# Row transposes that wait for each bank of the values by itself, and a value addition ahead of its slot's maxima

## The chip, the core and the metric

The kernel runs on one core of a Trainium2 chip, in one launch. The core's engines work side by side and each takes its own instructions in order: TensorE (PE, matrix products and transposes; its weight loads are shown apart as PEld), VectorE (DVE), ScalarE (ACT), GpSimd (POOL), and SyncE (SP), which issues DMAs. They wait for each other by semaphores. The metric is the device time of a launch in microseconds. A run is compared by its time, and the profiled execution is a run of its own.

## The reference: what is computed

16 images of 256 x 256 give 256 rows each (an edge filter of 2 x 2, clipped), and 77 text tokens are looked up as further rows, so that a batch element has 333 rows of 256. Then comes a layernorm, windowed attention with 16 heads of 16, a residual, a second layernorm and a mixture of eight experts, of which each row takes two.

```python
h = concatenate([tok(x), table[x_txt]], axis=1)
y = layernorm(h)
q, k, v = split_heads(y @ Wq + bq), split_heads(y @ Wk + bk), split_heads(y @ Wv + bv)
# windows of 128 rows at 0, 64, 128, 192, and a last one that ends at the last row
scores = q_win @ k_win.T * scale + pos_bias
merged = (sum over the windows of softmax(scores) @ v_win) / (windows that hold the row)
h = h + merged @ Wo + bo
x2 = layernorm(h)
top_scores, sel = top_k(softmax(x2 @ gate_w.T), 2)
h = h + scatter_add(top_scores * expert(sel)(x2))     # expert: (silu(x2 @ w1) * (x2 @ w3)) @ w2
```

## The kernel before, in words

There are two stages. The first goes over the 16 batch elements and does attention, the router, and the scattering of rows to the experts' slots in DRAM. The second (after about 740 us) works through the experts' tiles.

The first stage is a software pipeline in steps b = -3 to 17. In one step b the engines attend to batch element b, finish the element before it (b - 1: output projection, residual, second layernorm, router) and prepare the next ones (b + 1: q, k and v; b + 2: first layernorm; b + 3: image filter). Each step has 20 slots k, one for each group of four heads in each of five windows. The slot is the unit in which every engine's code is written: each engine has a loop over k, with the attention work of the slot and, hung on certain k, a piece of the other work. The order within each engine is therefore as it is written; no scheduler moves anything.

A group's attention work passes through the engines one or more slots apart: PE makes the scores of slot k (line 1105) into one of two banks of `s_bank`; DVE adds the bias and takes the negated maxima (line 818, four times, one per head, each with a short read of the accumulator; it signals `max_ready` after the fourth); ACT takes the exponentials of slot k - 1 (line 703, four times); PE transposes the probabilities of slot k - 3 (line 1116) into `t_bank`; ACT (line 696), for every fourth group DVE (line 827), copies them to `probsT`; PE multiplies those of slot k - 4 by the values (line 1132). PE's scores of slot k wait for the maxima of slot k - 2.

The work around the change happens in slots 12 to 18 and shares `m_bank`, two PSUM banks:

- PE makes the values of element b + 1 in three products (`v_proj`, line 1083): windows 0 and 2 into the two halves of bank 0 of `m_bank` (slots 12, 13), window 4 into bank 1 (slots 14, 15).
- DVE adds the bias `bv` to each and writes it to the values' tile (`add_v`, line 806, on the tile `v_all`). Each addition increments `v_ready`: the first two stand in slot 14 of DVE's code, the third in slot 16.
- In slot 15 DVE normalises the rows of element b - 1 (line 773, three instructions that write `rows`), once POOL has its inverse roots; in slot 16 those of element b + 2 (line 773, `xn`).
- In slot 17 PE transposes the normalised rows of element b - 1 into `m_bank` (line 1218): three transposes into bank 0 (c = 0) and three into bank 1 (c = 1). They overwrite the values' products, so they wait for the additions.
- ACT copies the transposed rows out in slot 18 (line 690, into the tile `rest`, which is x2T here), and PE multiplies them by the router's weights in its slot 18 (line 1225, 12 small products, `gate_out`). Behind these PE transposes the heads back (line 1091), and ACT copies them (line 722, `head_out`).
- SP waits for all three additions and then issues four DMAs (lines 412 to 416) that shift halves of the values between partitions, for windows 1 and 3. The first product of the next element reads them.

Of the kernel before, what the change touches and what calls it, by code (L numbers as in the profile page):

```python
# [54 lines left out]
def group_heads(g):  # L55

    return [8 * (g // 2) + g % 2 + 2 * i for i in range(GH)]


def build(nc, x, x_txt, table, Wq, bq, Wk, bk, Wv, bv, Wo, bo, pos_bias, gate_wT, w1, w2, w3, use, out):  # L60
    ctx = ExitStack()
    with ctx:
# [6 lines left out]
        def sem(name):  # L69
            return ctx.enter_context(nc.semaphore(name))  # L70
# [153 lines left out]
        v_ready = sem("v_ready")  # L224
# [88 lines left out]
        def has(b):  # L313

            return 0 <= b < B, 1 <= b <= B, 2 <= b <= B + 1, 0 <= b + 1 < B, 0 <= b + 2 < B, 0 <= b + 3 < B
# [434 lines left out]
        def _(dve):  # L750
# [19 lines left out]
            def normalise(src, first, dst, done):  # L770

                for j in range(NT):
                    dve.tensor_scalar(dst(j), src[:, j, :], moments[:, first + j, 0:1], rstd[:, first + j:first + j + 1],  # L773
                                      ALU.subtract, ALU.mult).then_inc(done, 1)

            def step(b, par):
                att, tail, tail2, proj, inp, pre = has(b)
                b9, b0, b1, b2, b3 = b - 2, b - 1, b + 1, b + 2, b + 3
# [22 lines left out]
                def add_v(n, w):  # L801
                    vt = v_win[1 - par]
                    dve.wait_ge(v_done, b1 * 2 + 1 + n // 2)
                    cols = vt[:, w, :].rearrange("p (t a e) -> p t a e", a=3, e=HD)[:, :, 0:3:2, :]
                    src = m_bank[:, n // 2, (n % 2) * D:(n % 2) * D + D]
                    dve.tensor_tensor(cols, src.rearrange("p (t a e) -> p t a e", a=2, e=HD),
                                      bv_row[:, :].rearrange("p (t a e) -> p t a e", a=2, e=HD),
                                      ALU.add).then_inc(v_ready, 1)

                for k in range(G):  # L810
                    if att:

                        g, r = k % NG, k % 4
                        dve.wait_ge(scores_done, b * G + k + 1)
                        if b * G + k >= 4:
                            dve.wait_ge(pT_done, b * G + k - 3)
                        for i, h in enumerate(group_heads(g)):
                            ins = dve.tensor_tensor_reduce(probs[:, r, i * WIN:(i + 1) * WIN],  # L818
                                                           s_bank[:, k % 2, i * WIN:(i + 1) * WIN], nbias[:, h, :],
                                                           1.0, BIG, ALU.add, ALU.min, neg_max[:, r, i:i + 1])  # L820
                        ins.then_inc(max_ready, 1)
# [125 lines left out]
                    if tail and k == 15:  # L947
# [2 lines left out]
                            dve.wait_ge(scattered, b0 * 96)  # L950
                            dve.wait_ge(x2T_done, b0)
                        normalise(hr, NT, lambda j: rows[:, 0, j, 0:D], rows0_ready)
                    if proj and k == 16:
                        add_v(2, 4)
                    if inp and k == 16:
                        dve.wait_ge(rstd_ready, b + 3)
                        if b2 >= 1:
# [2 lines left out]
                    if tail and k == 19:  # L960
# [6 lines left out]
                        for j in range(NT):  # L967
                            dve.wait_ge(best_ready, b0 * 6 + 1 + j)
                            dve.max_index(best_i[:, j, :], best[:, j, :], logits[:, j, :]).then_inc(best_ready, 1)

            run_steps(step)


# [78 lines left out]
        def _(pe):  # L1052
# [11 lines left out]
            def step(b, par):  # L1064
                att, tail, tail2, proj, inp, pre = has(b)
                b9, b0, b1 = b - 2, b - 1, b + 1
# [28 lines left out]
                for k in range(G):  # L1095
# [115 lines left out]
                        v_proj(1, 0, 4, 1)  # L1211
                    if tail and k == 17:
                        pe.wait_ge(rows0_ready, b0 * 3 + 3)
                        if proj:
                            pe.wait_ge(v_ready, b1 * 3 + 3)
                        for c in range(C):
                            for j, (t0, n) in enumerate(TILES):
                                mm = pe.transpose(m_bank[:, c, t0:t0 + n], rows[0:n, 0, j, c * P:(c + 1) * P],  # L1218
                                                  ident[0:n, 0:n])
                        mm.then_inc(x2T_done, 1)  # L1220
# [10 lines left out]
                    if (k - 5) % NG == 3 and ((att and v >= 0) or (tail and v < 0)):  # L1231
# [5 lines left out]
                        mm.then_inc(rawT_done, 1)  # L1237

            run_steps(step)


# [80 lines left out]
```

## Time and profile before

| | |
|---|---|
| median of 3 runs | 1263.39 us (1262.71 to 1264.84) |
| the profiled execution's own time | 1263.12 us |
| its span in the trace | 1261.2 us |
| mean granted TensorE clock | 0.973 of full speed |
| busy share of the span: PE, PEld, DVE, ACT, POOL | 91%, 75%, 66%, 56%, 47% |
| maxima on DVE (line 818), 1280 of them | 293.7 us, 285 ns each |
| exponentials on ACT (line 703), 1280 | 402.5 us, 398 ns each |

The shares are means over two unlike stages. In the second, from 750 us on, PE works nearly alone; the chain of waits that the page follows back from the end goes through it and says nothing of the first stage. For the first stage one has to look at the stretch from 60 to 720 us by itself, and in it at single slots: the timeline lists instructions in order of their start, neighbours of the same kind merged into one row with a count, and behind a row, in brackets, how long the engine had been idle before it and what released it. Instructions of one engine overlap a little at their ends, so the distance of two starts is shorter than the busy time of the first.

### The profile page before, as it was taken

What the parts mean: (1) busy time and instruction counts of PE and PEld (TensorE: products, weight loads), DVE (VectorE), ACT (ScalarE), POOL (GpSimd) and SP (SyncE); (2) the same over time, 40 slices, a digit from 0 to 9 for tenths busy, and PEclk for the clock granted to TensorE, in tenths of its full rate; (3) what the DMA queues carried; (4) which work ended last, traced back from release to release, by engine and by line L of the source; (5) the groups of instructions that cost most, each with busy time, mean ns of one, the idle gap of its engine ahead of it and who ended that gap; (6) DMA issues with size and microseconds to landing.
All of it is one profiled execution on the core that took longest, in us unless ns stands there. A gap on an engine that the chain in (4) does not pass through costs nothing. (4 is left out here: it accounts for less than half of the span.)

```text
span 1261.2 us, 34362 instructions
## 1 busy us (share of the span) xinstructions
PE 1149.9 (91%) x10510; PEld 946.9 (75%) x10511; DVE 837.0 (66%) x4259; ACT 706.7 (56%) x1977; POOL 594.6 (47%) x751
## 2 busy tenths in 40 slices
PE   2499999999999999999998449999999999999996
PEld 1367666766666766766666349999999999999995
DVE  3478989988998899998888444444444444444442
ACT  1399999999999999999999211111111111111110
POOL 7555656666567656765454323322332332232232
PEclk9799999999999999999999669999999999999998
DMA  5654445654354434533341533232323323323232
GB/s 135 172 159 138 139 136 167 172 149 129 116 150 138 115 100 140 160 107 87 113 135 35 162 110 47 48 50 46 49 47 49 47 46 50 46 46 50 46 50 30
DMA packets 98394, 123.31 MB, mean 98 GB/s; under 512 B 15544, under 2 KB 87416, under 8 KB 95192
## 3 DMA queue, kind: packets, MB, share of 16 engines
q1 hardware_dynamic: 75880, 89.96, 25.4%
q0 software_dynamic: 18576, 24.47, 11.5%
q10 hardware_dynamic: 3808, 7.34, 1.8%
q8 instruction: 59, 0.97, 0.3%
q14 instruction: 71, 0.58, 0.2%
HBM read 69.35 MB, written 46.07 MB: 92 GB/s over the span
## 5 line engine op out<-in xcount | busy, mean ns | idle before, releaser
L703 ACT ACTIVATE probs<-probs,neg_max 128x128 f32<-128x128 f32 x1280 | 402.5, 398 | 1.5 <-DVE neg_max L818 0.7
L818 DVE CUSTOM_DVE_ANT_0 probs<-s_bank,nbias 128x128 f32<-128x128 f32 x1280 | 293.7, 285 | 56.7 <-PE s_bank L1105 51.7
L741 ACT ACTIVATE v_all<-s_bank 128x512 f32<-128x512 f32 x91 | 54.4, 598 | 286.1 <-PE s_bank L1261 259.3
L1116 PE MATMUL t_bank<-ident,probs 128*128 128x128 f32 x1280 | 194.0, 274 | 0.2 <-ACT probs L703 0.2
L1276 PE MATMUL o_bank<-stacks,v_all 128*128 x728 | 172.4, 380 | 0.3 <-issue 0.2
L652 POOL DMA_INDIRECT out_dram<-wq_sb,nbias x46 | 75.9, 1651 | 194.3 <-DVE wq_sb L1026 172.7
L652 POOL DMA_INDIRECT out_dram<-wk_sb,nbias x45 | 73.3, 1629 | 175.0 <-DVE wk_sb L1026 172.1
L696 ACT ACTIVATE probsT<-t_bank 128x512 f32<-128x512 f32 x240 | 142.3, 593 | 20.7 <-PE t_bank L1116 18.5
L1032 DVE TENSOR_TENSOR v_all<-v_all,t_bank 128x512 f32<-128x512 f32 x91 | 62.6, 688 | 129.7 <-PE t_bank L1261 129.7
L1132 PE MATMUL o_bank<-probsT,v_all 128*32 128x128 f32 x2560 | 136.3, 285 | 7.3 <-ACT probsT L696 4.0
L1276 PEld LDWEIGHTS o_bank<-stacks,v_all 128*128 128x128 f32 x728 | 131.3, 190 | 15.4 <-issue 1.2
L1105 PE MATMUL s_bank<-stacks 96*128 96x128 bf16 x1280 | 126.0, 220 | 16.6 <-DMA stacks<-qk_parts 16.6
L1105 PEld LDWEIGHTS s_bank<-stacks 96*128 96x128 bf16 x1280 | 93.5, 98 | 59.7 <-issue 24.6
L1116 PEld LDWEIGHTS t_bank<-ident,probs 128*128 128x128 f32 x1280 | 134.4, 141 | 0.9 <-ACT probs L703 0.5
L523 POOL DMA_INDIRECT expert_slots<-rows,slot_i x96 | 97.5, 1016 | 44.7 <-issue 36.2
L735 ACT ACTIVATE v_all<-m_bank 128x256 f32<-128x256 f32 x91 | 35.0, 384 | 143.8 <-PE m_bank L1250 143.8
L818 DVE DVE_READ_ACCUMULATOR2_ANT neg_max<- 128x1 f32 x1280 | 104.9, 82 | 0.1
L1132 PEld LDWEIGHTS o_bank<-probsT,v_all 128*32 128x32 f32 x2560 | 50.3, 108 | 63.6 <-issue 45.1
L1261 PEld LDWEIGHTS s_bank<-v_all,probs 128*128 128x128 f32 x736 | 90.9, 195 | 3.2 <-ACT v_all L735 0.9
L1261 PE MATMUL s_bank<-v_all,probs 128*128 128x128 f32 x736 | 91.4, 278 | 0.5 <-ACT v_all L735 0.5
L1261 PE MATMUL t_bank<-v_all,probs 128*128 128x128 f32 x736 | 90.4, 276 | 0.0
L1261 PEld LDWEIGHTS s_bank<-v_all,parts_flat 128*128 128x128 f32 x720 | 87.4, 192 | 3.0 <-ACT v_all L735 0.7
(160 smaller groups left out, 1988.7 us busy)
## 6 DMA issues: line engine op xcount, KB each, us to landing
stacks<-qk_parts SPq DMA_DIRECT2D x192, 166.5 KB
qk_parts<-parts_flat SPq DMA_DIRECT2D x192, 83.2 KB
nbias<-expert_slots SPq DMA_DIRECT2D x91, 129.0 KB
w_sb<-in_L_ffn_w_dram ACTq DMA_DIRECT2D x14, 512.0 KB
v_all<-v_all SPq DMA_DIRECT2D x64, 96.0 KB
x_here<-in_x_dram SPq DMA_DIRECT2D x16, 256.0 KB
out_dram<-h_res SPq DMA_DIRECT2D x16, 256.0 KB
stacks<-in_L_ffn_w_dram SPq DMA_DIRECT2D x8, 512.0 KB
```

The lines of the kernel that those rows point to most:

```text
L523: pool.indirect_dma_start(slots_dram[:, :], bass.IndirectOffsetOnAxis(slot_i[0:n, kk, j:j + 1], 0), rows[0:n, kk, j, :], None).then_inc(sc ...
L652: pool.indirect_dma_start(out[:, :], bass.IndirectOffsetOnAxis(g_rows[r][:, D + 1:D + 2].bitcast(I32), 0), y_sb[r], None, compute_op=ALU.a ...
L696: act.activation(probsT[:, r, :], t_bank[:, r, :], ACT.Copy).then_inc(pT_by_act, 1)
L703: ins = act.activation(seg, seg, ACT.Exp, bias=neg_max[:, r, i:i + 1], scale=-1.0)
L741: act.activation(hidT[r % 2], s_bank[:, r % 2, :], ACT.Silu).then_inc(silu_ready, 1)
L818: ins = dve.tensor_tensor_reduce(probs[:, r, i * WIN:(i + 1) * WIN], s_bank[:, k % 2, i * WIN:(i + 1) * WIN], nbias[:, h, :], 1.0, BIG, AL ...
L1032: dve.tensor_tensor(hidT[r % 2], hidT[r % 2], t_bank[:, r % 2, :], ALU.mult).then_inc(hid_ready, 1)
L1105: mm = pe.matmul(s_bank[:, k % 2, i * WIN:(i + 1) * WIN], q_stack[par][0:KROWS, h, lo:lo + WIN], k_stack[par][0:KROWS, h, lo:lo + WIN], st ...
L1116: mm = pe.transpose(t_bank[:, (k - 3) % 2, i * WIN:(i + 1) * WIN], probs[:, r, i * WIN:(i + 1) * WIN], ident[:, :])
L1132: mm = pe.matmul(o_bank[32 * i:32 * i + 32, vp, g * WIN:(g + 1) * WIN], v_win[bp][:, w, c0:c0 + 2 * HD], probsT[:, (k - 4) % 2, i * WIN:(i ...
L1261: mm = pe.matmul(bank[:, par, n * P:(n + 1) * P], up_w[par][:, m, a, n * P:(n + 1) * P], gxT[par][:, a * P:(a + 1) * P], start=(a == 0), s ...
L1276: mm = pe.matmul(o_bank[:, r % 2, 0:D], hidT[r % 2][:, a * P:(a + 1) * P], w2_sb[:, bass.ds(e, 1), a, :].rearrange("p o n -> p (o n)"), st ...
```

## The change

Two things are edited. On DVE the third value addition, `add_v(2, 4)`, stood in slot 16 behind the four maxima of that slot; it now stands at the slot's beginning, before them. On PE the six row transposes of slot 17 waited once for all three additions; now the three into bank 0 wait for the first two (which read bank 0), and the three into bank 1 for the third.

```diff
--- before.py
+++ after.py
@@ -808,6 +808,8 @@
                                       ALU.add).then_inc(v_ready, 1)
 
                 for k in range(G):
+                    if proj and k == 16:
+                        add_v(2, 4)
                     if att:
 
                         g, r = k % NG, k % 4
@@ -950,8 +952,6 @@
                             dve.wait_ge(scattered, b0 * 96)
                             dve.wait_ge(x2T_done, b0)
                         normalise(hr, NT, lambda j: rows[:, 0, j, 0:D], rows0_ready)
-                    if proj and k == 16:
-                        add_v(2, 4)
                     if inp and k == 16:
                         dve.wait_ge(rstd_ready, b + 3)
                         if b2 >= 1:
@@ -1211,9 +1211,9 @@
                         v_proj(1, 0, 4, 1)
                     if tail and k == 17:
                         pe.wait_ge(rows0_ready, b0 * 3 + 3)
-                        if proj:
-                            pe.wait_ge(v_ready, b1 * 3 + 3)
                         for c in range(C):
+                            if proj:
+                                pe.wait_ge(v_ready, b1 * 3 + 2 + c)
                             for j, (t0, n) in enumerate(TILES):
                                 mm = pe.transpose(m_bank[:, c, t0:t0 + n], rows[0:n, 0, j, c * P:(c + 1) * P],
                                                   ident[0:n, 0:n])
```

DVE before, in a step with all the work, from the row normalisation of slot 15 to the maxima of slot 17 (in brackets the semaphores that an instruction waits for; ISA is the instruction of the maxima and its accumulator read; in the middle three more pairs of it are left out):

```order
L773 TENSOR_SCALAR rows<-h_res,moments,rstd 128x256 x2
L818 ISA probs,neg_max<-s_bank,nbias 128x128 [waits pT_done,scores_done]
L818 ISA neg_max 128x1
...
L806 TENSOR_TENSOR v_all<-m_bank,bv_row 128x8x2x16 [waits v_done]
L773 TENSOR_SCALAR xn<-h_in,moments,rstd 128x256 [waits xT_done,rstd_ready]
L773 TENSOR_SCALAR xn<-h_in,moments,rstd 128x256 x2
L818 ISA probs,neg_max<-s_bank,nbias 128x128 [waits pT_done,scores_done]
L818 ISA neg_max 128x1
```

DVE after, the same place (line 818 has become 820):

```order
L773 TENSOR_SCALAR rows<-h_res,moments,rstd 128x256 x2
L806 TENSOR_TENSOR v_all<-m_bank,bv_row 128x8x2x16 [waits v_done]
L820 ISA probs,neg_max<-s_bank,nbias 128x128 [waits pT_done,scores_done]
L820 ISA neg_max 128x1
...
L773 TENSOR_SCALAR xn<-h_in,moments,rstd 128x256 [waits xT_done,rstd_ready]
L773 TENSOR_SCALAR xn<-h_in,moments,rstd 128x256 x2
L820 ISA probs,neg_max<-s_bank,nbias 128x128 [waits pT_done,scores_done]
L820 ISA neg_max 128x1
```

The addition has moved past the four maxima and their reads, and keeps its wait for the values' product; the normalisation of `xn` now comes straight behind the maxima.

PE before, from the product of slot 13's group to the scores of slot 18:

```order
L1132 MATMUL o_bank<-probsT,v_all 32x128 [waits pT_by_act]
L1132 MATMUL o_bank<-probsT,v_all 32x128 x3
L1218 MATMUL m_bank<-ident,rows 128x128 [waits v_ready,rows0_ready]
L1218 MATMUL m_bank<-ident,rows 128x128
L1218 MATMUL m_bank<-ident,rows 128x77
L1218 MATMUL m_bank<-ident,rows 128x128 x2
L1218 MATMUL m_bank<-ident,rows 128x77
L1105 MATMUL s_bank<-stacks 128x128 [waits max_ready]
L1105 MATMUL s_bank<-stacks 128x128 x3
```

PE after:

```order
L1132 MATMUL o_bank<-probsT,v_all 32x128 [waits pT_by_act]
L1132 MATMUL o_bank<-probsT,v_all 32x128 x3
L1218 MATMUL m_bank<-ident,rows 128x128 [waits v_ready,rows0_ready]
L1218 MATMUL m_bank<-ident,rows 128x128
L1218 MATMUL m_bank<-ident,rows 128x77
L1218 MATMUL m_bank<-ident,rows 128x128 [waits v_ready]
L1218 MATMUL m_bank<-ident,rows 128x128
L1218 MATMUL m_bank<-ident,rows 128x77
```

No instruction has moved on PE. The first transpose still names `v_ready`, with a value lower by one, and the fourth has a wait of its own for the full count.

## Rows read from the trace of the kernel before

**Rows 1.** Busy time by stage: 60 to 380 us. Columns: us, engines' busy, clock, DMA.

```profile
60.00:380.00 320.00, 307.95 (x3269) 220.28 (x3268) 286.63 (x1868) 301.53 (x883) 198.34 (x281) 1.00 0.49 144
```

**Rows 2.** What PE waited for before the row transposes, line 1218: us, times.

```profile
  DVE v_all L806: 7.1, 11
```

**Rows 3.** Timeline, step 2 (longest wait): start us, busy us, engine, line, [idle before].

```profile
161.58 0.08 DVE L818 DVE_READ_ACCUMULATOR2_ANT neg_max<- 128x1 f32 x1
161.58 0.41 DVE L806 TENSOR_TENSOR v_all<-m_bank,bv_row 128x256 f32<-128x256 f32 x1
161.69 1.28 ACT L703 ACTIVATE probs<-probs,neg_max 128x128 f32<-128x128 f32 x4
...
162.14 0.77 PE L1218 MATMUL m_bank<-ident,rows 128*128 128x128 f32 x6 [0.95 <-DVE v_all L806]
...
162.94 0.73 ACT L690 ACTIVATE rest<-m_bank 128x666 f32<-128x666 f32 x1
...
163.86 1.33 PE L1225 MATMUL m_bank<-gate_sb,rest 128*128 128x8 f32 x12
```

**Rows 4.** Timeline, step 5 (short wait).

```profile
283.91 0.08 DVE L818 DVE_READ_ACCUMULATOR2_ANT neg_max<- 128x1 f32 x1
...
284.47 0.77 PE L1218 MATMUL m_bank<-ident,rows 128*128 128x128 f32 x6 [0.20 <-DVE v_all L806]
284.48 1.27 ACT L703 ACTIVATE probs<-probs,neg_max 128x128 f32<-128x128 f32 x4
...
285.65 0.71 ACT L690 ACTIVATE rest<-m_bank 128x666 f32<-128x666 f32 x1
...
286.42 1.33 PE L1225 MATMUL m_bank<-gate_sb,rest 128*128 128x8 f32 x12 [0.15 <-ACT rest L690]
```

**Rows 5.** Timeline of DVE alone, step 6, slots 15 to 17.

```profile
322.82 1.45 DVE L773 TENSOR_SCALAR rows<-h_res,moments,rstd 128x256 f32<-128x256 f32 x3 [0.24 <-POOL rstd L498]
324.19 0.28 DVE L818 CUSTOM_DVE_ANT_0 probs<-s_bank,nbias 128x128 f32<-128x128 f32 x1
...
325.03 0.08 DVE L818 DVE_READ_ACCUMULATOR2_ANT neg_max<- 128x1 f32 x1
325.03 0.41 DVE L806 TENSOR_TENSOR v_all<-m_bank,bv_row 128x256 f32<-128x256 f32 x1
325.37 1.05 DVE L773 TENSOR_SCALAR xn<-h_in,moments,rstd 128x256 f32<-128x256 f32 x3
...
327.18 0.08 DVE L818 DVE_READ_ACCUMULATOR2_ANT neg_max<- 128x1 f32 x1
```

**Rows 6.** Timeline of ACT alone, same stretch.

```profile
325.31 1.27 ACT L703 ACTIVATE probs<-probs,neg_max 128x128 f32<-128x128 f32 x4
326.48 0.71 ACT L690 ACTIVATE rest<-m_bank 128x666 f32<-128x666 f32 x1
327.29 1.28 ACT L703 ACTIVATE probs<-probs,neg_max 128x128 f32<-128x128 f32 x4
328.96 0.39 ACT L722 ACTIVATE head_out<-o_bank 128x256 f32<-128x256 f32 x1 [0.39 <-PE o_bank L1091]
```

**Rows 7.** Timeline of PE alone, same stretch.

```profile
324.59 0.43 PE L1132 MATMUL o_bank<-probsT,v_all 128*32 128x128 f32 x8
325.59 0.77 PE L1218 MATMUL m_bank<-ident,rows 128*128 128x128 f32 x6 [0.57 <-DVE v_all L806]
326.20 0.39 PE L1105 MATMUL s_bank<-stacks 96*128 96x128 bf16 x4
...
326.96 0.42 PE L1132 MATMUL o_bank<-probsT,v_all 128*32 128x128 f32 x8
327.32 1.33 PE L1225 MATMUL m_bank<-gate_sb,rest 128*128 128x8 f32 x12
```

**Rows 8.** Timeline of PE's weight loads, same stretch.

```profile
326.96 0.16 PEld L1132 LDWEIGHTS o_bank<-probsT,v_all 128*32 128x32 f32 x8 [0.17 <-issue]
```

**Rows 9.** Who waited for the row copy on ACT, line 690: us, times.

```profile
  PEld m_bank L1225: 6.5, 16
  PE m_bank L1225: 2.9, 6
```

## The prediction

> **What bounds the kernel now.** I began with the stages. The attention stage takes 60 to 720 us of the span, and in a stretch of it TensorE (PE) is busy 96%, ScalarE (ACT) 94% and VectorE (DVE) 90% [rows 1]. No one of them has room by itself. The clock is granted at 1.00 of full speed there, the 2.4 GHz level, so a wait on PE costs its own length and nothing more. The change touches one place per batch: the transposes of the outgoing rows (line 1218). The view of that line shows what PE waited for in front of it: 11 waits for the value addition on DVE (line 806), 7.1 us together [rows 2]. There are 16 such places, one per batch; the edit acts on 14 of them (in steps 1 to 14 both the row transposes and a next batch's values exist). Reading PE at each of the 14, I find ten waits of about half a microsecond or more, the longest of 0.95 us, one of 0.20 us [rows 3, 4], and three places without one. Ten waits share 7.1 - 0.2 = 6.9 us, 0.69 us each.
>
> A wait on PE is worth its length only if nothing else arrives at the same time. So I laid the three engines of one batch beside each other. On DVE [rows 5] the order is row normalisation, the four maxima of slot 16, the last value addition, three normalisations of the next batch, the maxima of slot 17. DVE runs through these without a gap. On ACT [rows 6] stand the probsT copy, the four exponentials of slot 16, the copy of the transposed rows (line 690), the exponentials of slot 17, and then a wait of 0.39 us for PE. On PE [rows 7] stand the transposes after 0.57 us of wait, then scores, one transpose group, one product, and at 327.32 the 12 router matmuls (line 1225), which need ACT's copy of line 690. Behind the router matmuls come the head transposes (line 1091) for which ACT waits, and the slots of the rest of the batch. So the router's start is the point that sets the time: everything after it in the batch follows at a fixed distance. From the router's start to ACT's head_out copy it is 328.96 - 327.32 = 1.64 us, with ACT idle just before, so nothing there absorbs a shift.
>
> **The change part by part.** It removes nothing and adds no arithmetic. It does two things.
>
> (a) On DVE the last value addition goes in front of the four maxima of slot 16. It takes 0.41 us, and its successor starts 325.37 - 325.03 = 0.34 us after it [rows 5]. So the maxima end 0.34 us later, at 325.03 + 0.08 + 0.34 = 325.45 instead of 325.11. What comes behind them doesn't move, since DVE does the same work without a gap either way. The addition's own operand is there: it needs the value product of slot 15, which stands ahead of slot 16's scores on PE.
>
> The Trainium skill (VectorE: DVE Perf Modes, "The DRAIN you can't avoid") says that the next operation doesn't start until the pipe is empty. By that the shift would be the full 0.41 us, and ten places would cost 0.7 us more than I count below. The trace of this case shows starts 0.07 us before the predecessor's recorded end, so I leave the rule aside.
>
> (b) On PE the first three transposes (bank 0) wait only for the first two additions, which DVE made in slot 14, and the other three for the last addition, which now ends at 324.19 + 0.41 = 324.60. PE needs neither wait any more. The product in front starts at 324.59, and PE goes on 0.36 us after such a start (326.96 to 327.32) [rows 7]. So the transposes start at 324.95, end their issue 0.61 us later (325.59 to 326.20 in the trace) at 325.56, and the scores of slot 18, which wait for the maxima of slot 16, start at 325.45 + 0.15 = 325.60 (0.15 us is what passed from the addition's end at 325.44 to the transposes at 325.59). From the scores to the router it is 327.32 - 326.20 = 1.12 us. PE would be ready for the router at 326.72, 0.60 us sooner than before.
>
> But now ACT is late. The exponentials of slot 16 started at 325.31, straight after the probsT copy; their maxima had ended at 325.11. With the maxima at 325.45, and 0.04 us from there to ACT (161.58 + 0.08 = 161.66 to 161.69 in the batch where ACT did wait [rows 3]), they start at 325.49. The copy of the rows follows 326.48 - 325.31 = 1.17 us later, takes 0.71 us, and the router starts 0.06 us after it (285.65 + 0.71 = 286.36 to 286.42, the batch where PE waited for exactly that [rows 4]). Sum: 325.49 + 1.17 + 0.71 + 0.06 = 327.43, against 327.32. The batch loses 0.11 us. The wait of 0.57 us isn't saved; it goes to the front of the router as 0.7 us.
>
> The ten places behave alike, because both paths are counted from the same instant, the end of addition and maxima together: before, 0.15 + 0.61 + 1.12 = 1.88 us through PE; after, 0.04 + 1.17 + 0.71 + 0.06 = 1.98 us through ACT. The batch with the longest wait [rows 3] gives 161.66 + 0.34 + 0.04 + 1.17 + 0.73 + 0.06 = 164.00 against 163.86, a loss of 0.14. Ten times 0.11 to 0.14 us is 1.2 us.
>
> The other four places cost nothing. In one of them [rows 4] the exponentials of slot 16 start at 284.48, and the maxima would end at 283.91 + 0.08 + 0.34 = 284.33, still in time; the router there waits for ACT already (0.15 us) and keeps its start, so the 0.20 us in front of the transposes aren't won either. The three places without a wait have ACT later still. If ACT were not late there, each would cost the same 0.14 us.
>
> The maxima of slot 17 end at 327.18 + 0.08 = 327.26 as before and their exponentials stand at 327.29 [rows 5, 6]. ACT's copy would now end at 327.37 and the exponentials start 0.1 us before such an end, so they stay. The four copies of values between partitions on SP's queue (DMAs) wait for the last addition and start some 0.8 us sooner; their reader is the first product of the next batch, eight slots on. Zero.
>
> The second wait inside the transposes, in front of the bank 1 half and with the scores of slot 18 queued behind it, is a thing that the trace doesn't show. Its lower bound is 0, its upper the 0.17 us by which weight loads on PE pause at the product of every slot (issue) [rows 8]. I take 0, because the 0.7 us in front of the router cover it. Were that cover gone, 14 times 0.17 would be 2.4 us.
>
> Sum: +1.2 us. The profiled execution took 1263.12 us (span 1261.2 and 1.9 around it), the median of the runs is 1263.39. So 1264.6 us.
>
> **The rivals.** First: PE sets the pace, and its waits are won. For it: PE has the highest busy share, and ACT waits for PE in every batch (0.39 us in [rows 6]). Then the 7.1 us go, and the time is 1256.3. It needs ACT's row copy to end by 326.66 instead of 327.19, so exponentials of slot 16 that start half a microsecond before their maxima end. That is against it. A smaller form, where PE's earlier scores let DVE do something sooner, wins some 3 us; but DVE has no gap in [rows 5]. The Trainium skill (Perfetto Trace Analysis, "Optimization Strategy") says to take the busiest engine, find its gaps and let what they wait for start sooner. By that rule alone this rival would be the forecast.
>
> Second, the slower side: the delay of the maxima reaches the router whole. The view of line 690 says that weight loads of the router waited for ACT's copy at all 16 places, 6.5 us together, and the matmuls at 6 [rows 9]. If the router was held by ACT and not by PE's queue at the ten places too, all that the exponentials lose counts: up to 0.34 us where ACT stood waiting [rows 3], ten times, 3.4 us, 1266.8. Against it: ten of the 16 router starts show no wait on PE's matmuls and come at the usual 0.36 us after the product. It decides from 0.25 us per place.
>
> Third: nothing moves. If the exponentials were held by something that isn't in my account by 0.2 us anyway, the loss is 0 and the time 1263.4.
>
> **How the numbers follow.** A measurement of this kernel tells 0.2%, 2.5 us, from no change. My forecast has 0.57, with a range of its own of 1263.0 to 1266.0; the first rival 0.17, the second 0.20, the third 0.06. Same is the forecast and the third, 0.63. Faster has the first but its smallest forms, 0.16. Slower has the second and the uncovered wait, 0.21. The range goes up to the second rival and the uncovered wait (1263.4 + 1.2 + 2.4 = 1267.0), say 1267.4, and down to the first one's half, 1259.8.
>
> **What would show it.** Right: in the changed profile the waits of line 1218 for line 806 are gone; the maxima of slot 16 end 0.34 us later behind the row normalisation; ACT waits for them before the exponentials; PE stands some 0.7 us in front of line 1225, released by ACT's line 690; the steps from row normalisation to router are 0.1 us longer. Wrong: if line 1225 starts sooner behind the row normalisation than before, ACT was not what I take it for; if it starts over 0.25 us later, the second rival holds; and if the batches' distance (40.8 us: [rows 3, 4] are three batches and 284.47 - 162.14 = 122.33 us apart) changes by more than the router's shift, something outside this place has moved, of which I have no account.

## The result

The change makes the kernel a little slower: 1266.81 us in the median (1264.74 to 1268.63, 20 runs) against 1264.59 (1262.71 to 1266.14, 20 runs). The ratio is 1.0019, with a 95% interval from 1.0012 to 1.0025; the medians differ by 2.2 us, and the interval is 1.5 to 3.2 us. The forecast was 1264.6 on a base of 1263.39, 1.2 us more. The base itself measures 1.2 us higher with more runs, and the change costs 1.0 us more than was said. Two executions, one of 5849 us of the kernel before and one of 2306 us in experiment 9, are in no ratio below. The profiled execution has a span of 1264.6 us (1261.2 before).

The waits for the value addition are gone. The first fence is the view of line 1218 of the changed kernel (what ended the idle time before it), the second that of line 690 (who waited for it); both answer to [rows 2, 9]:

```profile
  issue: 3.0, 15
```

```profile
  PEld m_bank L1225: 14.9, 16
  PE m_bank L1225: 10.6, 16
```

The 11 waits for line 806 no longer appear. But the router's matmuls now wait for ScalarE's row copy at all 16 places, 10.6 us together; it was 2.9 us at 6 places. What was saved in front of the transposes stands in front of the router. The timeline of step 2 of the changed kernel (start us, busy us, engine, line; the maxima are line 820 now) shows it in one place; it answers to [rows 3]:

```profile
159.80 0.40 DVE L773 TENSOR_SCALAR rows<-h_res,moments,rstd 128x256 f32<-128x256 f32 x1
...
160.12 0.41 DVE L806 TENSOR_TENSOR v_all<-m_bank,bv_row 128x256 f32<-128x256 f32 x1
...
160.46 0.28 DVE L820 CUSTOM_DVE_ANT_0 probs<-s_bank,nbias 128x128 f32<-128x128 f32 x1
...
160.74 0.80 PE L1218 MATMUL m_bank<-ident,rows 128*128 128x128 f32 x6
...
161.30 0.08 DVE L820 DVE_READ_ACCUMULATOR2_ANT neg_max<- 128x1 f32 x1
...
161.41 1.28 ACT L703 ACTIVATE probs<-probs,neg_max 128x128 f32<-128x128 f32 x4 [0.20 <-DVE neg_max L820]
...
162.60 0.70 ACT L690 ACTIVATE rest<-m_bank 128x666 f32<-128x666 f32 x1
...
163.35 1.34 PE L1225 MATMUL m_bank<-gate_sb,rest 128*128 128x8 f32 x12 [0.71 <-ACT rest L690]
...
164.99 0.38 ACT L722 ACTIVATE head_out<-o_bank 128x256 f32<-128x256 f32 x1 [0.49 <-PE o_bank L1091]
```

Take the end of the row normalisation, 159.80 + 0.40 = 160.20, as the zero (in the kernel before it is 160.81 at the same place). The addition comes first, then the maxima, which end at 161.38, 1.18 us after the zero against 0.85 before. The transposes start at 0.54 instead of 1.33. The exponentials start at 1.21, after 0.20 us of waiting for the maxima, the copy at 2.40, and the router at 3.15 behind 0.71 us of idle TensorE. In the kernel before it was 163.86 - 160.81 = 3.05. So the router is 0.10 us later. It is the same in all steps from 2 to 12: 3.15 us behind the zero, with 0.71 or 0.72 us of idle TensorE ahead of it. Before, it was 3.05 in ten of these eleven steps and 3.27 in step 5.

The other part wasn't in the forecast. Stretches of 41 us, about a step each (columns as in [rows 1]: length, busy PE, PEld, DVE, ACT, POOL, granted clock, DMA), of the changed kernel:

```profile
159.00:200.00 41.00, 39.59 (x418) 28.38 (x418) 37.25 (x242) 38.23 (x114) 26.69 (x38) 1.00 0.56 159
200.00:241.00 41.00, 40.13 (x409) 29.30 (x410) 36.94 (x241) 37.62 (x111) 25.89 (x35) 0.96 0.51 145
241.00:282.00 41.00, 39.97 (x413) 28.45 (x412) 36.19 (x234) 37.72 (x111) 26.02 (x35) 0.96 0.53 148
282.00:323.00 41.00, 39.98 (x408) 28.95 (x408) 36.76 (x240) 37.76 (x112) 25.92 (x34) 0.96 0.49 142
323.00:364.00 41.00, 39.56 (x420) 28.35 (x419) 37.28 (x242) 38.26 (x112) 26.72 (x37) 1.00 0.46 129
```

In three of them the mean granted clock is 0.96; in the kernel before all fourteen such stretches from 118 to 692 us have 1.00. One place by its instructions, TensorE alone:

```profile
246.24 1.34 PE L1225 MATMUL m_bank<-gate_sb,rest 128*128 128x8 f32 x12 [0.72 <-ACT rest L690]
...
247.90 0.84 PE L1116 MATMUL t_bank<-ident,probs 128*128 128x128 f32 x4
...
249.66 1.06 PE L1116 MATMUL t_bank<-ident,probs 128*128 128x128 f32 x4
...
252.67 0.61 PE L1116 MATMUL t_bank<-ident,probs 128*128 128x128 f32 x4
```

A group of four transposes that takes 0.61 us takes 0.84 to 1.06 us from 247.9 us on, and 0.61 again at 252.67: the granted clock is 0.50 from 248.2 to 251.5 us, the 1.2 GHz level, and some 3.4 us after its fall it is back at 2.4 GHz. The fall comes behind the 0.72 us of idle time and the router's twelve products of 8 columns, 1.9 us after the router's start; the other two, in steps 3 and 5, come 2.8 and 1.1 us after it. From router to router the three steps with such a fall take 41.87, 41.76 and 41.98 us, the steps without 41.02 as a rule (one has 41.23): 0.85 us for each fall. In all, from the router of step 2 to that of step 12, it is 412.93 us against 409.28, 3.65 us more: three falls of 0.85 are 2.55, and ten times 0.10 is 1.0.

### The profile page after: what moved, and what is told of

Read it like the earlier page. It is cut to its first block, busy times and chain, and to the rows that moved or that the text cites. A ratio compares the mean times of both kernels' runs of the same rounds, so it can differ in the third digit from the quotient of the medians.

```text
span 1264.6 us, 34362 instructions
## 1 busy us (share of the span) xinstructions
PE 1153.6 (91%) x10510; PEld 949.6 (75%) x10511; DVE 837.5 (66%) x4259; ACT 704.5 (56%) x1977; POOL 594.0 (47%) x751
## 4 chain that ended last, share of the span: by engine, by line
PE 73%; ACT 10%; POOL 5%; DVE 4%; issue 4%; SPq 2%; DMA 1%; ACTq 0%; POOLq 0%; DVEq 0%
PE s_bank L1261 13%; PE t_bank L1261 13%; PE o_bank L1276 12%; PE t_bank L1116 7%; PE m_bank L1077 6%; ACT probs L703 6%; PE o_bank L1132 5%; PE s_bank L1105 4%; PE m_bank L1071 3%; DVE probs L820 2%; PE m_bank L1083 2%; PE m_bank L1225 2%; PE o_bank L1235 2%; PE o_bank L1091 2%; PE m_bank L1250 2%
```

## The experiments

Each was timed in five rounds beside the kernel before. A difference in us is the ratio's, times the median of the kernel before; the difference of the two medians is up to 0.7 us away from it. I write "zero" for the end of the row normalisation in each kernel.

**1. The addition's move alone.**

```diff
 # the changed kernel, with TensorE's wait as it was
-                        for c in range(C):
-                            if proj:
-                                pe.wait_ge(v_ready, b1 * 3 + 2 + c)
+                        if proj:
+                            pe.wait_ge(v_ready, b1 * 3 + 3)
+                        for c in range(C):
```

> Only the move on VectorE: the last value addition ahead of slot 16's maxima; TensorE waits once for all three additions, as before the change. Theory (the path through ScalarE, and short falls of the clock): this is the whole of the change, so the router starts 3.15 us behind the row normalisation in ten steps (3.05 before), with 0.7 us of idle TensorE ahead of it, and the granted clock falls for 3.4 us now and then in the attention stage, 0.9 us each. 1265.5 to 1268. Rival (the second wait among the transposes costs): at least 0.5 us below the changed kernel, and the transposes' stretch shorter than there.

Measured: 1266.38 us (1264.21 to 1267.62) against 1263.85, ratio 1.0019 (1.0009 to 1.0029). The view of line 690:

```profile
  PE m_bank L1225: 10.6, 16
```

The same waits as in the whole change. The router is at 3.15 us in steps 2 to 12, and the clock falls twice in the profile. The move alone is the whole of the change, as far as the times can tell (the interval is 1.3 us to either side). The rival of a costly second wait is out by the traces: in the changed kernel TensorE isn't idle ahead of the fourth transpose in any of these steps, and from the first transpose to the fourth it is 0.34 or 0.35 us; here, with one wait for all, it is 0.31 to 0.35.

**2. The split wait alone.**

```diff
 # the kernel before, with the wait inside the loop; add_v(2, 4) stays behind the maxima
-                        if proj:
-                            pe.wait_ge(v_ready, b1 * 3 + 3)
                         for c in range(C):
+                            if proj:
+                                pe.wait_ge(v_ready, b1 * 3 + 2 + c)
```

> Only the split of the wait on TensorE: bank 0's transposes wait for two additions, bank 1's for the third; the third addition stays behind slot 16's maxima. Theory: the maxima are not late, TensorE wins some 0.3 us on its path, and ScalarE's path (2.93 to the end of the row copy, 0.06 to the router) allows 2.99 instead of 3.05 in six steps and 2.83 in the four where ScalarE had waited for the transposes. Sum -0.06 x 6 - 0.22 x 4 = -1.2 us, 1263.4, and fewer falls of the clock than in the changed kernel. Rival (TensorE's own queue sets the pace): -0.3 us in ten steps, -3 us. Other rival (the clock falls come with any kernel): falls here as in the changed kernel.

Measured: 1261.69 us (1260.29 to 1265.47) against 1263.85, ratio 0.9988 (0.9979 to 0.9997), 1.5 us less. TensorE in step 2:

```profile
160.78 0.51 PE L1218 MATMUL m_bank<-ident,rows 128*128 128x128 f32 x3
161.46 0.51 PE L1218 MATMUL m_bank<-ident,rows 128*128 128x128 f32 x3 [0.18 <-DVE v_all L806]
...
163.07 1.33 PE L1225 MATMUL m_bank<-gate_sb,rest 128*128 128x8 f32 x12
```

The first three transposes go ahead, the other three wait 0.18 us for the addition. With the maxima in time, the router starts at 2.84 us (163.07 less 160.22), 0.2 us sooner, now held by ScalarE's copy in steps 2 to 12 (I had taken 2.99 for six of them; with the steps more even, ScalarE comes earlier everywhere). One fall of the clock shows in this profile, so falls don't belong to the changed kernel alone. It comes in step 7, where TensorE had stood idle for 0.38 us ahead of the fourth transpose; in the other ten steps that is 0.17 to 0.20 us:

```profile
364.00:405.00 41.00, 40.25 (x412) 28.93 (x412) 36.67 (x241) 37.60 (x111) 26.65 (x37) 0.96 0.46 127
```

The two halves of the change have opposite signs: the split wait gains 1.5 us by itself, and the moved addition loses 2.4.

**3. The row copy ahead of the exponentials.**

```diff
 # the changed kernel, ScalarE
-                    if tail and k == 18:                     # stood at the slot's beginning
+                    if tail and k == (17 if att else 18):    # between the probsT copy and the exponentials
                         act.wait_ge(x2T_done, b0 + 1)
                         ...
                         act.activation(x2T[:, :, :], m_bank[:, :, 0:S], ACT.Copy).then_inc(x2T_ready, 1)
```

> The changed kernel, with ScalarE's row copy moved from slot 18 to slot 17, ahead of the exponentials of slot 16. Theory (ScalarE's exponentials and copy hold the router): the copy no longer waits for the exponentials, the router starts when TensorE comes to it, 2.45 us behind the row normalisation instead of 3.15, and about 0.5 us sooner in the late steps too; the exponentials of slot 16 end 0.7 us later, which their reader, five instructions behind the router, allows. 14 x 0.5 to 0.6 = 7 to 8 us below the kernel before, near 1257, and no fall of the clock. Rival (the delayed exponentials bite behind the router): the distance from router to head copy grows beyond 1.64 us and less than 3 us are won. Rival (TensorE or the row normalisation's distance from the last router sets the step): nothing is won.

Measured: 1260.08 us (1256.39 to 1261.95) against 1263.85, ratio 0.9968 (0.9958 to 0.9978), 4.0 us less: half of what was expected. TensorE and two rows of VectorE in step 2 (the zero is 161.53):

```profile
162.06 0.80 PE L1218 MATMUL m_bank<-ident,rows 128*128 128x128 f32 x6
...
163.89 1.33 PE L1225 MATMUL m_bank<-gate_sb,rest 128*128 128x8 f32 x12
165.29 0.44 PE L1091 MATMUL o_bank<-ident,ctx_q 128*128 128x128 f32 x2
...
166.73 0.43 PE L1132 MATMUL o_bank<-probsT,v_all 128*32 128x128 f32 x8 [0.34 <-DVE probsT L829]
```

```profile
164.74 0.49 DVE L848 TENSOR_TENSOR ctx_q<-o_bank,inv_sum 128x128 f32<-128x128 f32 x2
...
165.99 0.69 DVE L829 COPY probsT<-t_bank 128x512 f32<-128x512 f32 x1
```

The router does start without a wait, at 2.36 us, 0.8 us sooner than in the changed kernel. So ScalarE's exponentials and copy were what held it. But behind it the head transposes no longer follow at 1.19 us, but at 1.40, and the product of slot 15 waits 0.34 us for VectorE's copy. VectorE's work from the same zero hasn't become shorter, and is the next one late: `ctx_q`, which the head transposes read, ends at 3.70 us, and the copy starts at 4.46, as in the changed kernel. A chain that is relieved by 0.8 us gave back some 0.4 (steps of 40.5 to 40.7 us, without a fall, instead of 41.02). The profile also has three falls of the clock, in steps 5, 8 and 11. TensorE isn't idle ahead of the router here; each of these falls comes 3.0 us behind the router's start, some 0.5 us after the beginning of the idle time of 0.34 us that the first fence shows in step 2. One stretch with a fall:

```profile
282.00:323.00 41.00, 40.46 (x410) 29.32 (x410) 36.86 (x241) 37.91 (x112) 26.00 (x36) 0.96 0.51 145
```

Of its 9 runs 7 have a mean clock under 0.972.

**4. The idle time ahead of the router filled.**

```diff
 # the changed kernel, TensorE, transposes of slot k - 3
-                        for i in range(GH):
+                        for i in list(range(GH)) * (2 if proj and tail and k == 18 else 1):
                             mm = pe.transpose(t_bank[...], probs[...], ident[:, :])
```

> The changed kernel, with the four transposes of slot 15's probabilities made twice in TensorE's slot 18, just ahead of the router (the same values to the same place, no output changes). They take 0.54 us of the 0.72 us in which TensorE stands idle there. Theory (the falls of the clock come from that idle stretch ahead of the router's small products): the router stays at 3.15 us, idle time falls to about 0.2 us, the clock doesn't fall in the attention stage, and the kernel is 1 us over the one before, not 2.2; three late steps may cost 0.07 us each. Rival (the clock falls for another reason): falls as in the changed kernel, 1266 to 1268.

Measured: 1264.58 us (1262.62 to 1266.00) against 1263.85, ratio 1.0009 (1.0000 to 1.0018). TensorE in step 2 (zero 161.06), and three of the 41 us stretches:

```profile
162.53 1.04 PE L1116 MATMUL t_bank<-ident,probs 128*128 128x128 f32 x8
...
164.21 1.33 PE L1225 MATMUL m_bank<-gate_sb,rest 128*128 128x8 f32 x12 [0.28 <-ACT rest L690]
```

```profile
200.00:241.00 41.00, 40.00 (x425) 28.78 (x423) 37.27 (x241) 38.24 (x113) 26.63 (x38) 1.00 0.52 150
241.00:282.00 41.00, 39.99 (x424) 28.72 (x423) 37.11 (x240) 38.25 (x113) 26.65 (x38) 1.00 0.54 156
282.00:323.00 41.00, 40.06 (x424) 28.84 (x423) 37.54 (x243) 38.24 (x113) 26.63 (x38) 1.00 0.52 149
```

The idle time is down to 0.28 us, the router still at 3.15, and the clock is at 1.00 in all fourteen stretches. With more work the kernel is 1.1 us over the one before (0 to 2.3) instead of 2.4 (1.5 to 3.2). These intervals overlap, so the time alone doesn't show the gain; the clocks of the single runs do. Of its 11 runs none has a mean granted clock under 0.972 of full speed; of the changed kernel's 20 runs 13 have (1267.4 us on average, against 1266.1 for the other seven), of 29 runs of the kernel before beside it none. The mean over a whole run is a rough count of the falls: the profiles with three falls have 0.969, but that of experiment 6 has 0.972 with two, and that of experiment 2 has 0.973 with one, like the kernel before with none.

**5. The copy ahead, and some idle time filled.** The kernel of 3, and two transposes of slot 16's group made twice in slot 19.

```diff
+                        for i in list(range(GH)) + (list(range(2)) if proj and tail and k == 19 else []):
```

> The kernel with the copy ahead of the exponentials, and in addition two of the four transposes of slot 16's probabilities made twice in TensorE's slot 19, behind the router and the head transposes (the same values to the same place). They take 0.27 us of the 0.34 us for which TensorE waits there before the product of slot 15. Theory (short idle stretches next to the router's small products let the clock fall, 0.9 to 1.2 us each time): no fall in the attention stage, steps of 40.5 us throughout, 1257. Rival (the falls there come from the idle time before slot 17 or from elsewhere): three falls as in the kernel without it, 1260.

Measured: 1260.31 us (1259.03 to 1262.80) against 1264.92, ratio 0.9969 (0.9960 to 0.9979). The clock didn't fall, as expected, but the time is that of experiment 3, not 1257. The steps have become 40.5 to 40.9 us long (40.70 on average, against 40.58 for the steps of 3 without a fall): the additional work isn't hidden there, as it was in 4. By the times it took as much as the falls had; by the two profiles it took less (407.03 us from the router of step 2 to that of step 12, against 409.15), and no run here settles it.

**6. The same work elsewhere.** As 4, but the doubled transposes are those of slot 16 in TensorE's loop (`k == 16`), 5 us earlier.

> The changed kernel, with the four transposes of slot 13's probabilities made twice in TensorE's slot 16, where TensorE waits 0.32 us for ScalarE's raw copy, 5 us ahead of the router. The idle 0.72 us directly ahead of the router stay. Theory (it is the idle time next to the router that counts): two or three falls of the clock as in the changed kernel, 1266.8 or, if 0.2 us of the extra work shows, up to 3 us more. Rival (any additional work of TensorE in a step keeps the clock up): no falls, 1264.6.

Measured: 1267.91 us (1266.46 to 1269.55) against 1264.92, ratio 1.0026 (1.0016 to 1.0035). Three of its stretches:

```profile
159.00:200.00 41.00, 40.08 (x411) 29.10 (x409) 35.50 (x232) 37.49 (x110) 25.99 (x34) 0.96 0.53 156
200.00:241.00 41.00, 40.21 (x430) 28.96 (x430) 37.58 (x243) 38.53 (x113) 26.69 (x37) 1.00 0.51 146
241.00:282.00 41.00, 40.21 (x410) 28.90 (x407) 35.36 (x234) 38.14 (x112) 25.93 (x36) 0.96 0.52 152
```

Two falls in the profile, and 8 of 11 runs with a mean clock under 0.972. Additional work as such doesn't keep the clock up. The idle time ahead of the router didn't stay as it was, though: it is 0.72 us in four of the steps 2 to 12 and 0.39 in the other seven, where TensorE comes to the transposes later. Both falls stand in steps with 0.72.

**7. Half of the filling.** As 4, with two of the four transposes doubled; 0.50 us of idle time stay ahead of the router in six of the steps 2 to 12, and 0.41 in five.

> The changed kernel, with only two of the four transposes of slot 15's probabilities made twice ahead of the router: 0.27 us of the 0.72 idle us are filled, 0.45 stay. Theory: router start unchanged at 3.15 us, and falls rarer than in the changed kernel or none; 1264.6 to 1266.5. Rival (the second set's effect was chance): 1266.8.

Measured: 1267.36 us (1265.00 to 1271.05) against 1264.92, ratio 1.0016 (1.0007 to 1.0025). The profiled execution has three falls, all in steps with 0.50 us of idle time there; 3 of 11 runs have a mean clock under 0.972. No gain that could be told from the changed kernel, and a wide spread: inconclusive on how much idle time matters.

**8. The split wait, with the copy ahead.** The kernel of 2, with the edit of 3.

> The split of the wait alone (addition behind the maxima, as before), with the row copy ahead of slot 16's exponentials. Theory (two chains from the row normalisation: the copy needs the transposes, the exponentials the copy, and the head copy both): the second half of the transposes starts at 1.24 us behind the row normalisation and ends at 1.75, the copy ends at 2.50, eight exponentials follow, and ScalarE comes to the head copy at 4.74 us, against 4.69 in the kernel before, 4.48 with the split alone and 4.32 with the addition ahead. Ten steps 0.05 us longer, three late ones 0.15 us shorter: 1264 to 1265, no difference. Rival (the copy's place alone makes the gain): 1260, as in the kernel that has both.

Measured: 1257.81 us (1256.46 to 1259.37, only 5 runs) against 1264.25, ratio 0.9954 (0.9941 to 0.9967). This is the fastest version, 5.8 us (4.2 to 7.5) under the kernel before, and my expectation was wrong. TensorE, VectorE and ScalarE in step 2 (zero 160.09):

```profile
160.42 0.51 PE L1218 MATMUL m_bank<-ident,rows 128*128 128x128 f32 x3
161.32 0.51 PE L1218 MATMUL m_bank<-ident,rows 128*128 128x128 f32 x3 [0.40 <-DVE v_all L806]
...
162.79 1.33 PE L1225 MATMUL m_bank<-gate_sb,rest 128*128 128x8 f32 x12
163.98 0.42 PE L1091 MATMUL o_bank<-ident,ctx_q 128*128 128x128 f32 x2
```

```profile
163.30 0.49 DVE L846 TENSOR_TENSOR ctx_q<-o_bank,inv_sum 128x128 f32<-128x128 f32 x2
```

```profile
161.86 0.73 ACT L696 ACTIVATE rest<-m_bank 128x666 f32<-128x666 f32 x1 [0.99 <-PE m_bank L1218]
162.49 2.44 ACT L703 ACTIVATE probs<-probs,neg_max 128x128 f32<-128x128 f32 x8
164.82 0.37 ACT L722 ACTIVATE head_out<-o_bank 128x256 f32<-128x256 f32 x1
```

The copy ends at 2.50 us and ScalarE comes to the head copy at 4.73, as I had said. What was wrong is that this sets the step. It is the router at 2.70 us that does: from the router to the next row normalisation it is 37.9 us in the kernels of 1, 2, 4 and 8, whether the head copy comes 1.64 or 2.04 us behind it. The router comes 0.35 us sooner than before, TensorE isn't idle directly ahead of it, there is no fall of the clock in steps 2 to 12, and the steps take 40.58 us. The addition stays behind the maxima here, and the head transposes follow the router at 1.19 us: they come at 3.89 us, when `ctx_q` has ended (3.70, as in 3), so the longer distance of experiment 3 isn't there. By the profile 3.5 us of the gain lie between the routers of steps 2 and 12, and 2.1 in the three steps behind them.

**9. The copy ahead in the kernel before**, with nothing else.

> The kernel before, with nothing but the row copy ahead of slot 16's exponentials. Theory: the transposes start at 1.32 us and end at 2.09, the copy ends at 2.83, and ScalarE comes to the head copy at 5.06 us, 0.37 us later than in the kernel before, in ten steps; late steps gain 0.15. Sum +3 us: 1267 to 1268. Rival (the copy's place alone makes the gain): below 1262.

Measured: 1261.57 us (1260.07 to 1262.49 in eleven runs) against 1264.25, ratio 0.9980 (0.9972 to 0.9989). Wrong by the same error: the router stays at 3.05 us, and with it the ten steps (40.95 us on average, 40.93 before), though ScalarE is late at the head copy. The gain of 2.5 us comes, by the profile, from the steps in which ScalarE was late at the row copy: there the router comes 0.2 to 0.5 us sooner behind the zero, and the last three steps together are 2.1 us shorter, as in experiment 8. TensorE in step 2 (zero 160.32):

```profile
161.64 0.77 PE L1218 MATMUL m_bank<-ident,rows 128*128 128x128 f32 x6 [0.70 <-DVE v_all L806]
...
163.37 1.33 PE L1225 MATMUL m_bank<-gate_sb,rest 128*128 128x8 f32 x12
```

It stands idle 0.70 us in front of the transposes in this kernel, the router follows without a wait, and the clock doesn't fall in these steps: as much idle time ahead of the transposes was followed by none. The falls of the changed kernel came where the idle time stands right ahead of the router.

## Why the prediction was right, and where it fell short

The measured 1266.81 us lie above the forecast's own range (1263.0 to 1266.0) and inside the whole one (up to 1267.4) only by bounds that were set for two other causes, the second rival and the uncovered wait. As a difference to the kernel before, 2.2 us on the base of 1263.39, they would be 1265.6, in the forecast's own range. So it is in part luck that the number lies in the range: some 1.0 us of the extra time is what the sum counts, and the rest is a cost that it didn't have.

- **What bounds the kernel: right.** The router's start sets the step. Distances behind it stayed: router to head copy 1.64 us in the changed kernel as in [rows 6, 7], and so did the steps' length but for the router's own shift and the falls.
- **(a), the maxima 0.34 us later: right.** They end at 1.18 instead of 0.85 us, 0.33. The shift is the distance of two starts, not the 0.41 us of the instruction; here the maxima start at 160.46, 0.07 us before the recorded end of the addition (160.12 + 0.41). The Trainium skill (VectorE: DVE Perf Modes, "The DRAIN you can't avoid") says that the next operation doesn't start until the pipe has emptied, but also, in the same place, that one that isn't held starts earlier; the prediction named only the first half. It was right to go by the distance in the trace.
- **(b), TensorE ready 0.6 us sooner and then waiting 0.7 us: right.** The router waited 0.71 us for line 690, and experiment 1 shows that the split wait takes no part.
- **The sum through ScalarE, 0.04 + 1.17 + 0.71 + 0.06 = 1.98 us against 1.88: right.** 0.10 us in each of the ten steps, 1.0 us together. Experiment 4, where the clock stays up, costs 1.1 us with an interval from 0 to 2.3. The same sum for single batches gave 0.11 and 0.14 us, slightly high.
- **The places at no cost: nearly right.** In step 5 the router went from 3.27 to 3.15 us, a gain of 0.12. From router to router the last three steps changed from 40.79, 40.84 and 37.52 to 40.72, 40.71 and 37.22 us, 0.5 us less together. In them the router comes 0.1 to 0.3 us later behind the zero, and what follows it is shorter by 0.2 to 0.6. The steps ahead of these places had become more even; that this is the reason isn't shown. (The longest wait before was 0.98 us, in step 10, not the 0.95 of step 2; nothing rests on it.)
- **"A wait on PE costs its own length and nothing more": wrong.** This is the step that failed. It read the clock of 1.00 as given. The wait kept about its length when it moved (0.69 us on average before, 0.72 now), but it came to stand next to twelve small products, and there the granted clock fell to the 1.2 GHz level three times in the profiled run, 0.85 us each. The prediction's own sign for something outside its account, steps that change by more than the router's shift, came true in these three steps. In the timed runs falls come in some and not in others, which fits a median's loss (2.2 us) between 1.0 and the profile's 3.4.
- **The rivals.** The first (TensorE's waits are won) didn't happen, though experiment 2 gained 1.5 us with the split wait alone. The second (the delay whole, 3.4 us) has the right size for the profiled run and the wrong reason: the router is 0.10 us later, not 0.25.

That the falls of the changed kernel follow from the idle time ahead of the router is supported by 4 (filled there, none), 6 (filled elsewhere, two, both where 0.72 us had stayed) and 9 (0.70 us ahead of the transposes, none). It isn't a rule for all kernels here: the one fall of experiment 2 and the three of experiment 3 came with no such idle time, 0.1 us at most, but next to shorter idle stretches, 0.38 us ahead of the fourth transpose in 2 and 0.34 us behind the head transposes in 3; where the latter is filled (5) there is none. Runs with a mean clock under 0.972 are 4 of 9 in 1, 3 of 11 in 2, 7 of 9 in 3, and none in 5, 8 and 9. What stays open: why they came in three steps of the profiled run and not in the other eight with the same 0.72 us, how much idle time is too much (7 was inconclusive), and how the place and the length of idle time count together.

## What to carry to other kernels

When two chains start from one instruction and meet at another, a removed wait on one is worth only as much as the other is shorter; here it was longer by 0.10 us, because the instruction that was brought forward pushed the head of the other chain back. Look at what stands behind the instruction that you move ahead, and move off the second chain what doesn't belong to it: with the row copy ahead of the exponentials the split wait gained 5.8 us. The split wait alone gives 1.5 and the copy alone 2.5, so behind the moved copy the split is worth some 3.3 (an estimate from the two ratios, 5.8 less 2.5, each uncertain by more than 1 us). And where a wait is moved on TensorE, look at what it will stand beside.

## What the runs showed of the hardware

The granted clock of TensorE fell from the 2.4 to the 1.2 GHz level for 3.4 us at a time inside stretches in which TensorE is busy 97 to 99% of the time (40.0 to 40.6 of 41 us) and stands idle for no longer than 0.72 us at once. In the changed kernel each fall began 1.1 to 2.8 us after the start of twelve matmuls of 8 columns that stood behind 0.72 us of idle time, in three of eleven like places, and doubling four transposes (0.43 us more of work) in that idle time removed them all from the profile. Idle time of 0.69 to 0.92 us ahead of six transposes of 128 and 77 columns was followed by no fall (experiment 9), and idle time of 0.34 us 2.5 us behind the router's start by a fall in three of eleven steps (experiment 3).
